# Cross-attention with a routed FFN: a new call order with the scatters spread, the output bias on TensorE, the context delivered turned, and the first rows ahead of the set-up

## What is computed

```python
qh, kh, vh = proj(layernorm(x), Wq, bq), proj(ctx, Wk, bk), proj(ctx, Wv, bv)   # 16 heads of 16
scores = einsum('bhqd,bhkd->bhqk', qh, kh)
D_udps = (norm(qh)[..., :, None] + norm(kh)[..., None, :]) ** 2
attn = softmax(alpha * 4.0 * scores / D_udps)
x = x + einsum('bhqk,bhkd->bhqd', attn, vh) @ Wo + bo
probs = softmax(layernorm(x) @ Wr)                     # 8 experts
w, idx = top_k(probs, 2);  w = w / sum(w)
h = gelu(einsum('btd,edh->ebth', layernorm(x), W1) + b1)
out = x + sum over the two experts of w * (h @ W2 + b2)
```

## Time and profile before

| | |
|---|---|
| time, median of 3 | 1053.28 us (1051.5 to 1056.38) |
| profiled execution | 1048.44 us, of which the span of the trace is 1046.7 |
| mean granted clock | 0.938 |
| TensorE busy (weight loads) | 929.1 us, 89% (814.2) |
| VectorE, ScalarE, GpSimd busy | 688.0 us (66%), 637.1 (61%), 433.3 (41%) |
| indirect stores L1191 | 64, GpSimd 1,053 ns each |
| loads of rows and context, issue to landing | 3.6 and 2.1 us |

### The profile page before, as it was taken

The page is one execution under the profiler, slowest core; times in us unless marked ns, Lnnn a source line. Parts: engine busy times, 40 slices in busy tenths (PEclk is TensorE's granted clock), DMA queues, the critical chain, the costliest instruction groups (busy, mean ns, idle before and its releaser), DMA issues. The chain is left out here.

```text
span 1046.7 us, 30647 instructions
## 1 busy us (share of the span) xinstructions
PE 929.1 (89%) x10734; PEld 814.2 (78%) x10734; DVE 688.0 (66%) x1806; ACT 637.1 (61%) x1234; POOL 433.3 (41%) x572
## 2 busy tenths in 40 slices
PE   2699999998989979989988707999999999999994
PEld 1588887886877868868867506999999999999994
DVE  5357787785866857957758543566666666666663
ACT  0478888885966867858758403555555555555551
POOL 4235466556455564563544620233222222222222
PEclk9799999998998989989989757999999999999997
DMA  4202223122222332341332227433333333233322
GB/s 126 80 29 67 82 68 113 45 83 93 84 64 77 114 96 95 107 149 33 113 128 99 97 84 302 135 58 58 49 53 49 52 49 53 49 51 52 52 34 26
DMA packets 61893, 84.96 MB, mean 81 GB/s; under 512 B 9744, under 2 KB 55312, under 8 KB 59568
## 3 DMA queue, kind: packets, MB, share of 16 engines
q1 hardware_dynamic: 46976, 63.33, 18.9%
q0 software_dynamic: 13296, 18.00, 10.3%
q10 hardware_dynamic: 1472, 1.67, 0.6%
HBM read 49.99 MB, written 31.92 MB: 78 GB/s over the span
## 5 line engine op out<-in xcount | busy, mean ns | idle before, releaser
L1442 POOL DMA_INDIRECT out<-yw,rb x71 | 111.0, 1564 | 308.8 <-DVE yw L1413 228.5
L1375 ACT ACTIVATE h<-s_ps,b1t,inv 128x128 f32<-128x128 f32 x288 | 106.8, 458 | 89.8 <-PE s_ps L1326 88.9
L1375 ACT ACTIVATE h<-u_ps,b1t,inv 128x128 f32<-128x128 f32 x280 | 103.5, 461 | 87.4 <-PE u_ps L1326 86.6
L1396 DVE TENSOR_SCALAR hs<-h,hsc 128x512 f16<-128x512 f32 x142 | 69.3, 488 | 119.8 <-ACT h L1375 116.2
L647 ACT ACTIVATE pt<-gen,escale 128x512 f32<-128x512 f32 x128 | 85.7, 681 | 42.8 <-PE gen L433 21.3
L1398 DVE SCALAR_TENSOR_TENSOR hs<-h,hsc,hs 128x512 f16<-128x512 f32 x142 | 106.7, 751 | 5.1
L1326 PE MATMUL s_ps<-xt,w1s 128*128 128x128 f16 x1728 | 105.6, 221 | 2.6 <-issue 1.8
L1326 PEld LDWEIGHTS s_ps<-xt,w1s 128*128 x1728 | 100.7, 99 | 3.5 <-issue 3.0
L901 DVE SCALAR_TENSOR_TENSOR tw<-th,s_ps 128x1024 f32<-128x1024 f32 x64 | 77.9, 1218 | 38.2 <-PE s_ps L416 20.3
L1340 PE MATMUL pv_ps<-w2s_sb,hs 128*128 x864 | 100.6, 273 | 0.8 <-issue 0.7
L1326 PE MATMUL u_ps<-xt,w1s 128*128 128x128 f16 x1680 | 99.6, 219 | 0.0
(11 more groups left out here) (234 smaller groups left out, 1817.7 us busy)
## 6 DMA issues: line engine op xcount, KB each, us to landing
wl<-L_ffn_W SPq DMA_DIRECT2D x16, 1024.0 KB, 5.6
rb<-xrec SPq DMA_DIRECT2D x71, 132.5 KB
w2s<-wst SPq DMA_DIRECT2D x8, 1024.0 KB, 9.1
w2s_sb<-w2s SPq DMA_DIRECT2D x8, 1024.0 KB, 15.0
xin<-x SPq DMA_DIRECT2D x32, 128.0 KB, 3.6
cin<-ctx SPq DMA_DIRECT2D x32, 128.0 KB, 2.1
xres<-x SPq DMA_DIRECT2D x32, 128.0 KB, 4.0
out<-x SPq DMA_DIRECT2D x32, 128.0 KB, 2.0
```

Of the source, the lines that this page charges most:

```text
L1375: ins = act.activation(h32[n % HBANKS][:, m % HB, :], hbank[n % HBANKS][:, o:o + SLOT], ACT.Gelu, scale=inv1[:, bass.ds(ex, 1)].bitcast(F3 ...
L1396: dve.tensor_scalar(hi, h, scale, None, ALU.mult).then_inc(sig("hi"), 1)
L1442: pool.indirect_dma_start(out[:, :], bass.IndirectOffsetOnAxis(ap=rb[j][:, D + NE:D + NE + 1], axis=0), yw[s % 2][:, :], None, compute_op= ...
```

## The change

The second half and each pair's arithmetic stay, apart from the output's bias. Six things change in the first half.

1. **Order.** The five loops have a new order of calls, start at another `it`, and `TURNS` has a new order to match. `counts` is split from `shares` and stands ahead of it.
2. **Scatters.** `scatter(p)` with eight DMAs becomes `scatter(t, i, p)` with one, called eight times in two iterations, at five places.
3. **Context.** It is laid out turned (a reshape and transpose of the input array), `cin` has two buffers for each block, `norm` transposes the scaled rows only, `xct` is half as wide, and `project` reads `cin` for k and v.
4. **Output bias.** A matmul of `ones_b` with `bop` (three bf16 parts) starts the sum in `project_out`. `add_bias` and `xb` go, and `residual` adds `xres`.
5. **Set-up.** The first loads stand ahead of the weights', the first statistics ahead of VectorE's set-up and `norm(0, 0)`, `norm(1, 0)` ahead of most of GpSimd's. The copies of `uk` go to SP's queue. The rest of the set-up follows `means(1, 0)`, `norm(1, 0)` and `rows(0)`; the waits for it stand at its first users.
6. `kb` is computed behind the first half.

```diff
@@ TURNS
-    ("oc0", -2, "ote", 0), ("qte1", -1, "qte1", None), ("kte1", -1, "kte1", None), ("wo0", -2, "x10", None),
+    ("ex30", -1, "ex30", None), ("ex31", -1, "ex31", None), ("qte0", 0, "qte0", None), ("kte0", 0, "kte0", None),
...
@@ def sync_program(sp)
                 sp.dma_start(xin[b][:, :], x[row:row + P, :]).then_inc(sig(f"ldx{b}"), 16)
-                if p:
-                    sp.wait_ge(*at(f"xct{b}", p))
-                sp.dma_start(cin[b][:, :], c[row:row + P, :]).then_inc(sig(f"ldc{b}"), 16)
+                if p >= 2:
+                    sp.wait_ge(*at(f"v{b}", p - 1))
+                sp.dma_start(cin[b][:, p % 2, :, :].rearrange("q k t -> q (k t)"), c[row:row + P, :]).then_inc(sig(f"ldc{b}_{p % 2}"), 16)
...
+            load(0, 0)
+            load(1, 0)
+            for dst, src in ((wq_sb, wq), (wk_sb, wk), (wv_sb, wv)):
+                sp.dma_start(dst[:, :, :], src.rearrange("(k q) n -> q k n", q=P)).then_inc(sig("set_w"), 16)
...
+            sp.wait_ge(*at("set_pool", 2))
+            for b in range(2):
+                for i in range(b == 0, NSPLIT):
+                    sp.dma_start(uk[b][i * STRIP:(i + 1) * STRIP, :], uk[0][0:STRIP, :]).then_inc(sig("set_uk"), 16)
...
@@ def tensor_program(pe)
-                for i, src in enumerate((xn[b], cin[b])):
-                    for k in range(DC):
-                        o = (DC * i + k) * P
-                        ins = pe.transpose(g[:, o:o + P], src[:, k * P:(k + 1) * P], idf[:, :])
+                for k in range(DC):
+                    ins = pe.transpose(g[:, k * P:(k + 1) * P], xn[b][:, k * P:(k + 1) * P], idf[:, :])
...
+                if p == 0:
+                    biases()
+
+            def biases():
+                pe.wait_ge(*dma("set_late", 3))
+                pe.transpose(pv_ps[:, 0:NE * HC], b1r[:, :], idf[0:NE * HC, 0:NE * HC])
+                pe.wait_ge(*dma("set_b", 2))
+                for k in range(DC):
+                    ins = pe.matmul(pv_ps[:, P:P + D], bv_sb[:, k:k + 1].to_broadcast([P, P]), wo_sb[:, k, :],
+                                    start=(k == 0), stop=(k == DC - 1))
+                ins.then_inc(sig("set_bvo"), 1)
...
                 g = pe_turn(pe, f"wo{b}", p)
+                if p == 0 and b == 0:
+                    pe.wait_ge(*at("set_bo", 2 * NSPLIT))
+                pe.matmul(g[:, 0:D], ones_b[0:RROWS, :], bop[:, :], start=True, stop=False)
...
@@ def vector_program(dve)
+                if p == 0 and b == 1:
+                    set_biases()
+                    set_scales()
+                    set_buffers()
...
-                dve.tensor_tensor(x1[b][:, :], turn(f"wo{b}", p)[:, 0:D], xb[b][:, :], ALU.add).then_inc(sig(f"x1{b}"), 1)
+                dve.tensor_tensor(x1[b][:, :], turn(f"wo{b}", p)[:, 0:D], xres[b][:, :], ALU.add).then_inc(sig(f"x1{b}"), 1)
...
@@ def gpsimd_program(pool)
+                if p == 0 and b == 1:
+                    set_selectors()
...
-            def add_bias(b, p):
-                pool.wait_ge(*dma(f"ldr{b}", p + 1))
-                if p:
-                    pool.wait_ge(*at(f"x1{b}", p))
-                pool.tensor_tensor(xb[b][:, :], xres[b][:, :], bo_sb[:, :], ALU.add).then_inc(sig(f"xb{b}"), 1)
...
-            def scatter(p):
+            def scatter(t, i, p):
                 m = p // 2
+                pool.wait_ge(*at("rtok", m + 1))
                 pool.wait_ge(*at("ridx", m + 1))
                 for b in range(2):
                     pool.wait_ge(*at(f"rl{b}", p + 1))
-                for t in range(4):
-                    for i in range(2):
-                        pool.indirect_dma_start(xrec_d[:, :], bass.IndirectOffsetOnAxis(ap=idx[:, i, t:t + 1], axis=0),
-                                                rec[m % 2][:, t, :], None).then_inc(sig("scat"), 16)
+                pool.indirect_dma_start(xrec_d[:, :], bass.IndirectOffsetOnAxis(ap=idx[:, i, t:t + 1], axis=0),
+                                        rec[m % 2][:, t, :], None).then_inc(sig("scat"), 16)
...
```

More of the change, by code:

```diff
@@ L91, in build @@
     turns = [(what, it + d, freed, (it + d) // 2 + 1 if what == "rank" else it + d + 1 if b is None else 2 * (it + d) + b + 1)
[L92 removed]
+             for it in range(-2, NP + 3) for what, d, freed, b in TURNS
              if 0 <= it + d < NP and (what != "rank" or (it + d) % 2)]
@@ new lines, in tensor_program @@
+                if 0 <= it < NP:
+                    scores(3, it)
+                    values(0, it)
+                    weight_sum(it)
+                    turned(1, 1, it)
+                if 0 <= it - 1 < NP:
+                    turn_y(1, it - 1)
+                if 0 <= it < NP:
+                    turned(2, 0, it)
+                if 0 <= it + 1 < NP:
+                    rows(it + 1)
+                if 0 <= it < NP:
+                    values(1, it)
+                if 0 <= it + 2 < NP:
+                    norm(0, it + 2)
@@ L578, in tensor_program @@
+                if 0 <= it < NP:
+                    turned(2, 1, it)
+                if 0 <= it - 1 < NP:
+                    logits(1, it - 1)
+                if 0 <= it + 2 < NP:
+                    norm(1, it + 2)
+                if 0 <= it < NP:
+                    heads_back(0, it)
+                    values(2, it)
             g = pe_turn(pe, "cnt", 0)
             pe.wait_ge(*at("racc", NP // 2))
+            pe.matmul(g[:, NE:2 * NE], ones_f[:, :], b1ss[:, :], start=True, stop=True)
@@ L1023, in weight_exponent @@
                 dve.tensor_scalar(wsc[:, :], wkk[:, :], -float(ONE), 268.0 * ONE, ALU.mult, ALU.add).then_inc(sig("wsc"), 1)
-            for it in range(-3, NP + 2):
+            for it in range(-2, NP + 3):
                 if 0 <= it - 1 < NP:
                     heads_back(0, it - 1)
-                    weight_exponent(it - 1)
+                if 0 <= it - 3 < NP and it % 2 == 0:
+                    shares(it - 3)
+                    positions(it - 3)
+                if 0 <= it - 2 < NP and it % 2:
+                    choose(it - 2)
+                if 0 <= it + 2 < NP:
+                    means(0, it + 2)
+                if 0 <= it - 1 < NP:
+                    weight_low(it - 1)
+                if 0 <= it - 2 < NP and it % 2:
+                    counts(it - 2)
                 if 0 <= it < NP:
```

580 lines of the change are left out of this document (285 added, 295 removed), and 14 rows, old and new, of the table TURNS.

## The result

The changed kernel takes 997.19 us (median of 4, 995.65 to 997.98) where the kernel before takes 1053.99 (median of 4, 1051.5 to 1056.38): a ratio of 0.946, with a 95% interval of 0.9434 to 0.9485. The forecast was 1002, the range 982 to 1028. The profiled execution took 997.15 us with a span of 995.4; the excess of the median over the profiled execution, 4.8 us before, is gone.

What follows compares the result with a forecast made beforehand. TensorE was taken to bound each pair, with its signals late during scatter bursts. Scatters -37.3, context and bias -3.3, order +4.5, start -9.4, end -3 sum to -48.5: 1048.4 becomes 999.9, plus half the median's excess 1002 us; range 982 to 1028.

Steps and rivals of the forecast that it cites:

- the scatters: In the long pairs: issuing the eight scatters spread out, not in one burst, gains 37.3 us (bounds 22 and 43).
- What a spread group still costs: In pairs with scatters: each of six spread groups still costs 1.0 us, bounds nothing and 3.5 us.
- the first rival: Scatter groups still hold TensorE three us or more, the clock falls, long pairs stay: 1039 us, chance 0.11.
- The new order: TensorE's calls reordered in each pair: waits lose 0.3 us a pair, 4.5 us in all (bounds 0 and 15).
- some 31 us: Floor for a pair's length, because TensorE has the same calls in another order.
- VectorE's chain ahead of `turned(0,0)`: At a pair's beginning: VectorE needs some 10.8 us, TensorE has 9 to 10.5 us of work, so waits of some tenths.
- Context and bias: Per pair on TensorE: four transposes fewer gain 0.44 us, two bias matmuls cost 0.22; net gain 3.3 us in all.
- Start: Before the first pair: rows scaled earlier bring the first score product to 37.7 us, gaining 9.4 (bounds 5 and 13).
- End: Last pair and way to the second half: a gain of 3 us (bounds 0 and 7).
- my three steps: At the end: values copy's wait gains 3 us, `counts` ahead of `shares` 0.7; work ahead of the last residual costs 1.
- the clock fell: Slower rival: VectorE's chain three us longer idles TensorE, lowering the clock in every pair: 1116 us, chance 0.05.
- The Trainium skill's rule: Objection in the scatter term: scatters cannot hold TensorE, so spreading them would not help; 1039 us, as the first rival.

Runs made afterwards that it cites:

- before_spread2: Kernel before with only its eight scatters spread one by one between GpSimd's other calls, on a chip with late signals: 1009.20 us against 1052.25, ratio 0.9585.
- before_spread: Kernel before with only its eight scatters spread one by one, on a chip where the kernel before takes 1006.37 us: 1007.96 us, ratio 1.0015.
- four_transposes: Changed kernel with two more, unread transposes of the scaled rows in each norm, four a pair: 999.95 us, ratio 0.9491 to the kernel before.
- eight2_loads: Changed kernel with scatters at eight places of one pair and the second pair's rows and context loaded before SP's wait for the selectors: 977.52 us, ratio 0.9282.
- before_again: Kernel before, unchanged, run again for its trace, on a chip without late signals: 1006.57 us, ratio 1.0001.
- row8: Changed kernel with its eight scatters in one row again, ahead of split_max(0), on a chip without late signals: 1019.53 us, ratio 1.0126 to the kernel before.
- eight2: Changed kernel with its scatters at eight separate places, all within one pair, on a chip without late signals: 982.97 us, ratio 0.9764 to the kernel before.

## Why the prediction was right, and where it was not

The time came out 5 us beside the forecast, and the term that carries it, the scatters, is shown. That it came so close is partly luck: two errors of some 9 us cancel, and the chip was one with late signals.

**What bounds the kernel.** TensorE bounds the pair, and the long pairs come from late signals in the rows of eight: shown by before_spread2, where the spread alone took the fifteen pairs from 512.1 to 472.3 us. I had put this at the chance of 0.73 without knowing that it holds on some chips only. On the two others the loss is missing before the change, and the forecast of -37.3 us for it would have been wrong there by all of it (before_spread: 1.6 us slower with the spread).

**Scatters and order together.** Forecast: -37.3 - 3.3 + 4.5 = -36.1 us over the pairs. Measured: -36.7. The sum is right because its terms err against each other. The scatters gave back 28.5 us, not 37.3: of the 43.3 us of excess the five pairs keep 14.8. The rest of the pairs' gain, 8.2 us, is order, context and bias, for which the forecast was a loss of 1.2.

- What a spread group still costs was taken as 1.0 us, between 0 and 3.5. The five pairs with scatters are 2.95 us longer than their neighbours, so this was the mis-sized term, three times too small. Half of it is the late signal in the row of three (1.6 us), as the first rival had feared for that row, but without the fall of the clock. The other half (1.4 us) is a wait that the prediction did not have: the two scatters at the end of a pair stand ahead of `split_max(0)`, and one of them runs into `weight_low`.
- The new order was taken as a loss of 0.3 us a pair. Pairs without scatters went from 31.4 to 30.5, or 30.9 with `choose` or `counts` in them; 0.22 of that is the context (four_transposes), -0.08 the bias, so the order gains some 0.8 us in the one kind and 0.4 in the other. The floor of "some 31 us" for a pair was wrong with it: TensorE's 30.4 busy of 31.4 us left a us of waits, and in the new order about half of that is left (30.05 of 30.5). VectorE's chain ahead of `turned(0,0)`, which I had counted as just as long as TensorE's work, made TensorE wait nowhere in a pair without scatters.
- Context and bias: forecast 0.2 us a pair, measured 0.22 - 0.08 = 0.14. Both single prices, 0.44 and 0.22, were two to three times too high: in these two cases the next row's start overstates what the short matmuls are worth to a pair.

Some numbers of the prediction were slightly off, with no weight in the result: 16 x 0.22 is 3.5 and not 3.3, and the upper bounds of all terms together would have come to 1036 us and more, beyond the range. In the earlier trace rows the signal of 307.50 is not the first late one: VectorE read the score product that ended at 306.46 only at 309.03.

**Start.** Forecast -9.4, measured -12.0. The steps up to the rows came out nearly as written: loads issued at 20.05 (forecast 19.4), statistics of p = 1 at 22.84, squares of both blocks done at 25.6 (25.5), `rows` at 28.23 (29). Timelines of VectorE and TensorE in the changed kernel, to be set beside the earlier trace rows:

```profile
4.10 0.43 DVE L849 BATCH_NORM_STATS2 ln_st<-xin 128x6 f32<-128x256 f32 x1 [2.80 <-DMA xin<-x]
...
22.84 0.43 DVE L849 BATCH_NORM_STATS2 ln_st<-xin 128x6 f32<-128x256 f32 x1 [7.08 <-issue]
...
28.23 0.66 PE L373 MATMUL gen<-idb,ar 128*96 128x128 bf16 x4 [9.69 <-DVE ar L900]
...
33.22 1.06 PE L413 MATMUL u_ps<-uk,aq 99*128 99x512 bf16 x2
35.12 1.05 PE L425 MATMUL s_ps<-kt,qt 32*128 32x128 f32 x14
```

The step that failed is the last: I carried 3 us from the factors to the scores over from before, plus 1 for the biases. It is 1.9 here with nothing added. The rows show `stack` of the first block ahead of the factors now, and the bias products (28.82 to 31.19) between `rows` and the factors, where TensorE waited 3.16 us before; which of the two saves how much was not tried. That the loads behind the selectors hold the start up was right: eight2_loads took 4.2 us more off it.

**End.** Forecast -3, measured -2.7, with the second half unchanged. The ranks come 44.8 us behind the last pair's first score product instead of 49.4 (the earlier trace rows lie in this stretch), and the first records of the second half come 24.3 us behind the ranks instead of 22.2. Which of my three steps this is was not tried.

**Rivals.** The long pairs did not stay, and the clock fell in no pair after the first. The Trainium skill's rule that TensorE and ScalarE never wait on anyone (SBUF — State Buffer, section "SBUF: two separate sides") would, as I had read it, have given 1039 us. The traces of before_again and row8 agree with that reading: no signal of TensorE is late beside rows of eight. Those of the kernel before and of the changed kernel do not: 7.6 and 3.1 us. But my reading went further than the section, which speaks of the ports of SBUF: a late semaphore signal is not shown to be a wait at such a port, so the runs refute my inference and not the rule.

**What stays open.** What differs between the chips isn't known. All runs on one chip were made together, so that they do not tell the chip from anything else that stayed the same meanwhile. How often either kind occurs isn't known either. It is not the pace of the scatters: away from `weight_low` one takes GpSimd 0.96 to 1.10 us in a row of eight on both kinds, and the mean packet of its queue in the first half took 0.13 and 0.12 us. Nor is it shown what in a row of scatters delays a signal of TensorE.

## What to carry to other kernels

Issue indirect stores one at a time between other work, behind the small operations that TensorE waits for and not ahead of one (eight2 and eight2_loads have neither of the two waits); before moving one, list everybody who waits for it to land, not only the queue that it stands in. Time a change on more than one chip, each beside the kernel before: here the same two kernels stood at 0.946 and at 0.979. Price a short instruction by adding it and reading the length of a whole period, not by the start of the row behind it.

## What the runs showed of the hardware

- The same program took 1006.4 and 1006.6 us on two chips and 1052.3 to 1054.0 on others. By one profile of each kind the whole difference lies in the fifteen pairs (512.1 against 469.6 us), five of which are long: late semaphore signals of TensorE beside rows of indirect stores, and the half clock after the idle time that they make. Signals of the other engines were not late.
- Where signals come late, the longest delay grows with the row: 0.4 to 0.6 us for single stores, 1.1 for two in a row (seen once), 3.1 for three, 7.6 for eight.
- An indirect store that started while VectorE's `weight_low` ran held GpSimd for 3.19 us instead of 0.97, until 0.98 us after `weight_low` had ended. GpSimd's cast of 2.18 us ended with `weight_low` as well.
- In row8 the clock stood at its lower level for 6.8 us behind an idle time of 3.89 us (38.2 us for a pair); waits of 1.4 and 1.6 us in one pair of the changed kernel left it at its upper level.
